# Preparation batch by batch with four banks, and a second attention with three banks for row maxima and scores in six parts a pair

## What is computed

```python
x = x + L0_xattn(layernorm(x), ctx, ctx, mask, Wq, Wk, Wv, Wo)     # 16 heads of 64
x = x + L0_ffn(layernorm(x), ...)                                  # each of 8 experts takes its best tokens
x = x + L1_xattn(layernorm(x), ctx, ctx, Wq, bq, ..., Wo, bo)      # 16 heads of 16, band of 128
x = x + L1_ffn(layernorm(x), ...)                                  # one group of 2 experts a token

# inside L1_xattn
scores = einsum('bhqd,bhkd->bhqk', qh, kh) / 4
scores = where(abs(pos_q - pos_k) <= 128, scores, -inf)
w = softmax(scores); out = einsum('bhqk,bhkd->bhqd', w, vh) @ Wo.T + bo
```

## Time and profile before

| | |
|---|---|
| median of 3 runs | 1455.58 us (1453.64 to 1457.38) |
| the profiled execution, its own time | 1457.49 us |
| its span, first to last instruction | 1455.6 us |
| PE, DVE, ACT, POOL busy | 79%, 55%, 42%, 35% of the span |
| preparation | 0 to 53.2 us, PE busy 8.5 us |
| second attention | 907 to 1162 us, first product 923.96 us |

### The profile page before, as it was taken

The page is one execution under the profiler, slowest core; times in us unless marked ns, Lnnn a source line. Parts: engine busy times, 40 slices in busy tenths (PEclk is TensorE's granted clock), DMA queues, the critical chain, the costliest instruction groups (busy, mean ns, idle before and its releaser), DMA issues. The chain is left out here.

```text
span 1455.6 us, 29951 instructions
## 1 busy us (share of the span) xinstructions
PE 1149.4 (79%) x10895; PEld 857.2 (59%) x10896; DVE 797.6 (55%) x2325; ACT 615.9 (42%) x1074; POOL 505.9 (35%) x490
## 2 busy tenths in 40 slices
PE   0589999999999998337999266587988743888896
PEld 0256777777777776335888223355655442777775
DVE  3357787787778785757110253367677441444443
ACT  3167787687677774200312022143444311322331
POOL 3265545445444241300444230989000013011012
PEclk9989999999999999655899769699999956999999
DMA  6122222222312120700355414455111042111010
GB/s 231 51 51 68 64 55 63 65 51 64 78 45 66 47 57 11 261 1 9 115 158 169 108 66 167 136 158 166 44 39 46 2 149 70 23 26 26 13 21 8
DMA packets 80169, 110.87 MB, mean 76 GB/s; under 512 B 11504, under 2 KB 58352, under 8 KB 79664
## 3 DMA queue, kind: packets, MB, share of 16 engines
q1 hardware_dynamic: 69584, 88.23, 20.7%
q0 software_dynamic: 10464, 21.01, 6.3%
HBM read 59.86 MB, written 24.70 MB: 58 GB/s over the span
## 5 line engine op out<-in xcount | busy, mean ns | idle before, releaser
L520 DVE CUSTOM_DVE_ANT_0 masked<-sc,mask_bias 128x512 f32<-128x512 f32 x256 | 175.5, 686 | 57.2 <-issue 40.3
L496 DVE TENSOR_TENSOR e_t_lo<-et,e_t_hi 128x512 f16<-128x512 f32 x256 | 176.6, 690 | 50.2 <-ACT e_t_hi L462 47.9
L469 ACT ACTIVATE e<-masked,neg_max 128x512 f32<-128x512 f32 x256 | 184.1, 719 | 27.3 <-DVE neg_max L520 26.8
L462 ACT ACTIVATE e_t_hi<-et 128x512 f16<-128x512 f32 x256 | 152.0, 594 | 88.0 <-PE et L413 87.5
L413 PEld LDWEIGHTS et<-ident,e 128*128 128x128 f32 x1024 | 125.7, 141 | 54.1 <-ACT e L469 6.3
L413 PE MATMUL et<-ident,e 128*128 128x128 f32 x1024 | 154.1, 273 | 1.4 <-ACT e L469 0.7
L1243 ACT ACTIVATE d_e<-d_st 128x768 f32<-128x768 f32 (+1 forms) x96 | 83.9, 882 | 121.6 <-PE d_st L1328 108.4
L175 PE MATMUL h_hb<-h_xt_hi,experts_hi 128*128 128x256 f16 x352 | 101.5, 288 | 26.6 <-DVE h_xt_lo L1708 26.6
L175 PE MATMUL ob<-v_hi,e_t_hi 128*128 128x65 f16 x1024 | 119.0, 193 | 0.6 <-DVE e_t_lo L496 0.6
L176 PE MATMUL ob<-v_lo,e_t_hi 128*128 128x65 f16 x1024 | 119.2, 193 | 0.0
L177 PE MATMUL ob<-v_hi,e_t_lo 128*128 128x65 f16 x1024 | 118.4, 193 | 0.0
(11 more groups left out here) (315 smaller groups left out, 2894.6 us busy)
## 6 DMA issues: line engine op xcount, KB each, us to landing
kk<-nat_k SPq DMA_DIRECT2D x128, 128.0 KB, 2.4
raw<-in_fc SPq DMA_DIRECT2D x16, 1024.0 KB, 6.5
qq<-nat_q SPq DMA_DIRECT2D x128, 64.0 KB, 2.0
mask_raw<-in_mask SPq DMA_DIRECT2D x16, 256.0 KB, 2.9
scratch_stack<-c_qk_hi SPq DMA_DIRECT2D x32, 128.0 KB
scratch_stack<-c_qk_lo SPq DMA_DIRECT2D x32, 128.0 KB
d_expert_raw<-in_gate_w POOLq DMA_DIRECT2D x8, 512.0 KB, 4.8
d_expert_raw<-in_up_w POOLq DMA_DIRECT2D x8, 512.0 KB, 4.1
```

The costliest lines, as they stand in the source:

```text
L462: nc.scalar.activation(e_t[u % NBUF].hi[:], et[u % 2][:], ACT.Copy).then_inc(turned_hi, 1)
L469: nc.scalar.activation(e[u % NBUF][:], masked[u % NBUF][:], ACT.Exp, bias=neg_max[:, g % 2, j:j + 1], scale=-1.0).then_inc(exp_ok, 1)
L496: nc.vector.tensor_tensor(e_t[u % NBUF].lo[:], et[u % 2][:], e_t[u % NBUF].hi[:], ALU.subtract).then_inc(turned_lo, 1)
L520: nc.vector.tensor_tensor_reduce(masked[u % NBUF][:], sc[j % 2][:], mask_bias[g // PAIRS % 2][:, j % QT, :], -SCALE0, 3e38, ALU.add, ALU.m ...
```

## The change

It edits two phases and nothing else.

In the preparation x is loaded in four transfers, one a batch, each with its own semaphore, and the statistics of a batch wait for its quarter alone. There are four PSUM banks and eight `z` buffers in place of two and four. Each weight has its own semaphore, and wk comes first. On ACT the eight bank copies stand ahead of the weights; the context copy is cut into two halves, behind the second and the fourth bank copy. POOL subtracts the context in the same two halves, and then makes the lo of wv; DVE makes those of wk, wq and wo.

In the second attention three single banks each serve the maxima and the scores. The pieces are the same matmuls; the scores of a pair come in six parts of one bank (four of 384 columns, two of 512), and PE's list alternates one piece of the maxima with one part of the scores.

```diff
-        z = [sb(f"z{i}", [P, D]) for i in range(4)]
-        bank = [ps(f"zt_bank{i}", [P, DT, 2 * P]) for i in range(2)]
+        z = [sb(f"z{i}", [P, D]) for i in range(NZ)]          # NZ = 8
+        bank = [ps(f"zt_bank{i}", [P, DT, 2 * P]) for i in range(NBANK)]   # NBANK = 4
@@ SP
-                sp.dma_start(T.x[:], dram["x"].rearrange("(t p) d -> p t d", p=P)).then_inc(x_in, 16)
+                for b in range(B):
+                    sp.dma_start(T.x[:, b * QT:(b + 1) * QT, :], ...).then_inc(x_in[b], 16)
@@ ACT
-                act.wait_ge(ctx_in, 16)
-                nc.scalar.activation(T.ctx_t.hi[:], ctx_raw[:], ACT.Copy).then_inc(ctx_hi, 1)
-                act.wait_ge(w_in, 64)
-                for i, w in enumerate(weights):
-                    nc.scalar.activation(...)
-                for g in range(NT // 2):
-                    act.wait_ge(zt_done, g + 1)
-                    nc.scalar.activation(T.z_t.hi[...], bank[g % 2][:], ACT.Copy).then_inc(zt_hi, 1)
+                for g in range(NT // 2):
+                    turned_part(g)
+                    if g in (1, 3):
+                        ctx_part(g // 2)
+                for i, w in enumerate(weights):
+                    act.wait_ge(w_in[i], 16)
+                    nc.scalar.activation(flat(w.hi), w_raw[i][:], ACT.Copy).then_inc(w_hi, 1)
@@ DVE
-                    if t % 2 == 1 and t >= 3:
-                        zt_lo_part(t // 2 - 1)
+                    if t % 2 == 1 and t >= 5:
+                        zt_lo_part(t // 2 - 2)
@@ second attention
+WORKS, PARTS = 3, 6
-        wk = [ps(f"d_wk{i}", [P, 512]) for i in range(2)]
-        st = [ps(f"d_st{i}", [P, 2, 512]) for i in range(2)]
+        wk = [ps(f"d_wk{i}", [P, 512]) for i in range(WORKS)]
+        st = [ps(f"d_st{i}", [P, 512]) for i in range(3)]
@@ SP
-                        sp.wait_ge(st_full, 3 * (n - QBUF + 1))
+                        sp.wait_ge(st_full, PARTS * (n - QBUF + 1))
@@ PE
-                    if f >= 2:
-                        pe.wait_ge(work_free, f - 1)
+                    if f >= WORKS:
+                        pe.wait_ge(work_free, f - WORKS + 1)
@@ PE, scores
-                    if f >= 2:
-                        pe.wait_ge(exp_ok, f - 1)
-                    places = ...
+                    if f >= 3:
+                        pe.wait_ge(exp_ok, f - 2)
+                    for kt, col in (((1, 0),), ((2, 0),), ((0, 0), (QT - 1, 2 * P)))[i % 3]:
+                        mm = banded_scores(n, st[f % 3], a, kt, col, k, q)
@@ PE, a slot
+                    for i in range(PARTS):
+                        if first:
+                            maximum(slot, i)
+                        if mid:
+                            scores(slot - 2, i)
+                        if i == 1 and 1 <= slot <= PAIRS1:
+                            shift_turn(slot)
+                        if i == 3 and slot % 2 == 0 and 0 <= slot // 2 - 2 < QUADS:
+                            attend(slot // 2 - 2)
+                        if i == 3 and slot % 2 == 1 and 0 <= slot // 2 - 2 < QUADS:
+                            turn_heads(slot // 2 - 2)
```

More of the change, by code:

```diff
@@ L75, in phase_prepare @@
 def phase_prepare(nc, sem, sb_x, T, dram):
+    NBANK, NZ = 4, 8
     with ExitStack() as ctx:
@@ L92, in phase_prepare, with flat @@
         z_done, zt_done, zt_hi, zt_lo = sem("z_done"), sem("zt_done"), sem("zt_hi"), sem("zt_lo")
-        weights = [T.wq0, T.wk0, T.wv0, T.wo0]
+        weights = [T.wk0, T.wq0, T.wv0, T.wo0]
+        WK, WQ, WV, WO = range(4)
+        def flat(part):
+            return part[:].rearrange("p c n -> p (c n)")
         with nc.Block() as block:
@@ L109, in _ @@
                                    pattern=[[-1, P]], channel_multiplier=1).then_inc(ident_ok, 1)
[L110 to L114, removed]
+                for c in range(DT):
+                    pool.wait_ge(ctx_hi, c + 1)
+                    pool.tensor_tensor(T.ctx_t.lo[:, c, :], ctx_raw[:, c, :], T.ctx_t.hi[:, c, :], ALU.subtract)
@@ L116, in _, with turned_part, ctx_part @@
+                pool.wait_ge(w_hi, WV + 1)
+                pool.tensor_tensor(flat(T.wv0.lo), w_raw[WV][:], flat(T.wv0.hi), ALU.subtract)
             @block.scalar
             def _(act):
+                def turned_part(g):
+                    act.wait_ge(zt_done, g + 1)
+                    nc.scalar.activation(T.z_t.hi[:, :, g * 2 * P:(g + 1) * 2 * P], bank[g % NBANK][:], ACT.Copy).then_inc(zt_hi, 1)
+                def ctx_part(c):
+                    act.wait_ge(ctx_in, 16)
+                    nc.scalar.activation(T.ctx_t.hi[:, c, :], ctx_raw[:, c, :], ACT.Copy).then_inc(ctx_hi, 1)
@@ L124, in _ @@
-                for g in range(NT // 2):
-                    act.wait_ge(zt_done, g + 1)
-                    nc.scalar.activation(T.z_t.hi[:, :, g * 2 * P:(g + 1) * 2 * P], bank[g % 2][:], ACT.Copy).then_inc(zt_hi, 1)
+                    act.wait_ge(w_in[i], 16)
+                    nc.scalar.activation(flat(w.hi), w_raw[i][:], ACT.Copy).then_inc(w_hi, 1)
             @block.vector
             def _(dve):
-                dve.wait_ge(x_in, 16)
-                layernorm_stats(nc, dve, T, 0, T.x, stats, mv, sd)
+                for b in range(B):
+                    dve.wait_ge(x_in[b], 16)
+                    for t in range(b * QT, (b + 1) * QT):
+                        nc.vector.bn_stats(stats[:, t, :], T.x[:, t, :]).then_inc(T.stat_done, 1)
@@ L132, in _ @@
+                dve.wait_ge(T.stat_done, NT)
+                for t in range(NT):
+                    nc.vector.bn_aggr(mv[:, t, :], stats[:, t, :]).then_inc(T.mv_done, 1)
+                dve.wait_ge(T.mv_done, NT)
+                nc.vector.tensor_scalar(sd[:], mv[:, :, 1], EPS, None, ALU.add).then_inc(T.var_eps, 1)
+                dve.wait_ge(T.sd_done, 1)
                 nc.vector.reciprocal(rstd[:], sd[:]).then_inc(rstd_done, 1)
@@ L1238, in _ @@
                         act.wait_ge(pv_done, m - EBUF + 1)
-                    for i in range(3):
-                        f = 3 * n + i
+                    for i in range(PARTS):
+                        f = PARTS * n + i
                         act.wait_ge(st_full, f + 1)
-                        src = st[f % 2][:, :, 0:3 * P] if i < 2 else st[f % 2][:].rearrange("p a (w s) -> p a w s", w=2)
-                        nc.scalar.activation(part(e[m % EBUF][:, 2 * half:2 * half + 2, :, :], i), src, ACT.Exp, scale=SCALE1).then_inc(exp_ok, 1)
+                        src = st[f % 3][:, 0:3 * P] if i % 3 < 2 else st[f % 3][:].rearrange("p (w s) -> p w s", w=2)
+                        nc.scalar.activation(part(e[m % EBUF][:, 2 * half + i // 3, :, :], i % 3), src, ACT.Exp, scale=SCALE1).then_inc(exp_ok, 1)
                     if half == 0 and m >= 1:
```

80 lines of the change are left out of this document (29 added, 51 removed).

## The result

The change took 1429.01 us, the median of 4 runs (1428.48 to 1433.4), beside 1455.49 for the kernel before: ratio 0.9825, 95% interval 0.9802 to 0.9848. Forecast were 1428: by the medians it is 26.5 us less where 27.5 were worked out, by the ratio, which is formed from all runs of both kernels and not from their medians, 25.5 (22 to 29). The profiled execution's span is 1427.3 us. All times and ratios here are of fast runs; one slow run of e12 (1666.78 us at a granted clock of 0.715, the others 0.892 to 0.900) is left out.

A forecast was written before the change was run, and what follows sets the result against it. The preparation was taken to be bound by an order, the second attention by PE, stopping once a slot. Savings of 9.5 and 18.0 us, 27.5 together, gave 1430.0 profiled and 1428 against the median; range 1423 to 1434, chance 0.50.

The forecast's parts named there:

- Preparation, 9.5 us less: Preparation: with earlier statistics and reordered copies and subtractions, the phase ends at 43.7 instead of 53.2, 9.5 us less.
- The bound that the trace of before did not show: Preparation: DVE's SBUF subtraction beside POOL's is either not held (end 40.6) or held (43.7); held was taken.
- three rows with DVE held: Preparation: evidence cited against the rival that less is held there (chance 0.22, 1425 or 1419).
- The third bank removes the stop at the boundary: Second attention, slot boundary: with three banks PE's wait for DVE's reduction goes, 0.65 us a slot.
- The fourteen even slots 4 to 30: Second attention: each even slot shrinks by 0.70 us, 9.8 together.
- Odd slots, 0.55 less: Second attention: odd slots lose the 0.65 wait but PE waits 0.1 for the split's transfer; six give 3.3.
- The five from 5 to 13: Second attention: odd slots set by a late split transfer shrink by 0.40 us each, 2.0 together.
- the second rival: Second attention: the split's transfer, queued behind a 256 KB load, lands later and costs 9 us; 1437, chance 0.19.
- the prediction's own sign of being wrong: Second attention: odd slots near 4.9 with PE waiting for the split's transfer, or the DVE wait returning elsewhere.
- First three slots, closings, tail, 2.9: Second attention: these and slot 31 together give 2.9 us less, an estimate between 0 and 5.
- The whole attention, 18.0: Second attention: sum of even slots, odd slots and the remaining stretches, 18.0 us less.
- Exponentials, hidden: Second attention, ACT: six exponentials for three add 17 us, hidden behind PE; the uncovered case had chance 0.03.

The follow-up runs named there:

- e12: The change with the turned maxima between first and second part of the scores, and no GpSimd subtractions in the preparation: 1422.95 us, ratio 0.9807.
- e10: The change with GpSimd's first half of the context held back until all sixteen z are made: 1425.35 us, ratio 0.9809.
- e3: The change with PE's list in the order of before, keeping three banks and six score parts: 1429.33 us, ratio 0.9826.
- e6: The change with two work banks in place of three, the alternating order kept: 1436.56 us, ratio 0.9888.
- e9: The change without the loads of q and k after pair 3 in the second attention: 1422.17 us, ratio 0.9797.
- e4: As e3, but SP's load waits also for the last piece of the maxima of its slot: 1431.08 us, ratio 0.9833.
- e5: The kernel before, run once more with nothing changed: 1454.4 us, ratio 1.0014.
- e1: The change's preparation with the second attention of the kernel before: 1439.28 us, ratio 0.9909.
- e2: The preparation of the kernel before with the change's second attention: 1436.83 us, ratio 0.9875.
- e8: The change with GpSimd's subtractions in the preparation all given to VectorE: 1426.06 us, ratio 0.9813.

## Why the prediction was right, step by step

- **Preparation, 9.5 us less:** right, 10.0 in the rows. First z 12.80 (12.7), POOL's halves from 18.14 (18.2), one z held by each, wk's hi from 30.67 (30.9). The bound that the trace of before did not show was taken at the right end: two subtractions from SBUF exclude each other (wo 5.16; e10). The prediction counts three rows with DVE held; the earlier trace rows have one each. The rule of the Trainium skill (SBUF — State Buffer, Who interferes with whom) holds here for the subtractions. The traces add that an instruction that waits gets in as soon as the other's present one ends, so each of two z, which read one tensor from SBUF, was held for one half.
- **The third bank removes the stop at the boundary:** right, and in even slots more came, 0.87 for 0.70. The rest was a second, small stop that the sum had not seen: before, the piece behind the turned maxima started 0.27 us after them (1112.81 to 1113.08), now 0.11 (1073.49 to 1073.60). The bank does this too without the alternation: e3 has the 0.11 and the 6.22, and e6, with two banks, 0.46 to 0.54. The waits for reductions fell from 25 to 5. The fourteen even slots 4 to 30, closings included, took 11.1 us less, for 9.8.
- **Odd slots, 0.55 less:** this step failed. The six that the sum counts (15 to 27 without 21) took 4.93 on the mean (4.98, 5.43, 4.49, 4.35, 5.04, 5.28), and 4.94 before: 0.1 us in all for 3.3. The five from 5 to 13, from which 2.0 were to come, took 31.2 for 30.6. The working was right for a slot without a wait (4.35). What it left out is the landing of the load itself: the prediction has its later issue (5.3 us after the turned maxima in even slots), but asks only what it does to the split behind it. In slots 25 and 27 the load was late by 0.67 and 0.91. In 15 and 17 the split was late by 0.75 and 1.07, and without loads (e9) still by 0.76 and 0.89. So odd slots stayed near 4.9, as the second rival had it and as the prediction's own sign of being wrong says, but not by that rival's mechanism: slot 19, e4 and e9 speak against a split delayed by the load ahead of it. Its price was 9; the odd slots fell short by 5.5.
- **First three slots, closings, tail, 2.9:** closings gave 1.1 each (9.75 to 8.63) and the slots after them 1.0 (9.87 to 8.84), more than I had counted; both are in the 11.1 above. The first slots' 7.4 are mostly chance (e5).
- **The whole attention, 18.0:** from the first product to the next phase the trace of before has 238.7 us and that of the change 219.1, so 19.7 less: even slots 11.1, odd ones 0.2 more, the first three 7.4, the rest 1.3. Over executions it is less: 238.7, 235.2 and 229.1 (before, e5, e1), mean 234.4, against 219.1, 214.1, 220.5 and 219.7 (change, e2, e8, e10), mean 218.3: 16 us. Too much for odd slots, too little for even ones and closings. That the total came within 2 us of the forecast is in part luck: the odd slots fell short by 5.5, the even ones brought 1.3 more, and the chance of the first slots fills the rest in the profiled pair.
- **Exponentials, hidden:** right; 494 and 598 ns (495 and 600). The trace puts three waits of PE down to them, 1.8 us in all, and one of the three, 0.67, was a load's.

## What to carry to other kernels

Where a stop is taken away, look for the transfer that has the least slack behind it: it sets what is left. Look at each transfer's own landing, and not only at what it does to the one behind it. Subtractions from SBUF that are shared out between VectorE and GpSimd took here the sum of both: add the two up before moving one to the engine that looks idle. And before a term is put down to a change, let the same code run twice; here half of a phase scattered by 10 us and the other half by 0.1.

## What was not expected of the hardware

The clock's rise came 4, 9 or 11 us after PE resumed, in executions of the same code. From the first product to the fourth turned maxima these took 20.1, 21.8 and 27.7 us, but most of that spread is not the clock's: 4.5 us of it are PE's waits, at full clock, for the split's transfer of slots 2 and 3: it took 5.0 us from DVE's end, and 2.54 in the quiet slots of e3 and e4. POOL's 4.05 us subtraction and DVE's 2.2 exclude each other so strictly that leaving the faster one alone with all six pieces ended the phase 4.8 us sooner.
